# Attention, product of the probabilities with the values: key tiles 2, 3 before 0, 1, and the two row sums placed anew

## The chip, the core and the metric

The kernel runs on one core of one Trainium2 chip. The metric is the time of the whole program on the device in microseconds (us): before the change the median of three runs is 1252.38 us (1252.17 to 1255.42).

## What is computed

The reference is one block of a network on x of shape 8 x 512 x 128: a feed-forward part with routed experts, attention, and the same feed-forward part again. The change touches attention alone. Cut to what matters:

```python
b, n, _ = x.shape                     # 8, 512, 128;  HEADS = 16, DIM_HEAD = 64
qkv = x @ w_qkv.T
q, k, v = jnp.split(qkv, 3, axis=-1)  # each turned to (b, heads, n, 64)
q = q * cos + rotate_half(q) * sin + fenc
k = k * cos + rotate_half(k) * sin + fenc
dots = jnp.einsum('bhid,bhjd->bhij', q, k) * scale
attn = jax.nn.softmax(dots, axis=-1)
out = jnp.einsum('bhij,bhjd->bhid', attn, v)
return out @ w_out.T + b_out
```

## The kernel before

Attention goes in 64 steps, one for each of 8 batches times 8 pairs of heads. Such a step is called g. The five engines run a software pipeline of periods p = 0 to 63. In period p the work of several steps is under way: query and key of step p + 3 are projected and rotated, those of p + 2 are finished, the row maxima of p + 1 are taken, the scores of p are begun and those of p - 1 ended, p - 1 is multiplied with the values, and the output of p - 3 is projected and added to x. Every engine has its own list of instructions, written out by hand and kept in order by counting semaphores; nothing is reordered by a scheduler.

The probabilities of a step lie in `work` (`pt`): 4 tiles of 128 keys, each 128 x 1024 (both heads, 512 queries each). They serve twice. TensorE multiplies them with the values (`apply_v`, line 1184, 4 key tiles by 2 heads, 16 rows in the trace). And their sums over all keys are the softmax's denominators. For these, VectorE adds tile 1 onto tile 0 (`first_sum`, line 1383) and GpSimd adds tile 3 onto tile 2 (`second_sum`, line 1463), in place, so each may start only when `apply_v` has read its tiles. Then TensorE sums tiles 0 and 2 over the partitions (`denominators`, line 1201). `apply_v` signals `first_applied` behind its second tile and `o_ps` behind its last.

What else the period holds, by engine and in its order:

- TensorE: `apply_v` of p - 1 (L1184); the turn of the maxima of p + 1 (L1136); in every eighth period four transposes of the next batch (L1087); the projections of query and key of p + 3 (L1093); a tile of values (L1020); the output projection of p - 3 (L1211); `denominators` of p - 1 (L1201); then, as the first rows of the next period, four rounds of a product for the maxima (L1012) and one of scores (L1161, L1166). The second round of L1012 writes the bank that the output projection has left its result in, and so waits for VectorE's residual sum (`y_done`); the third and fourth wait for maxima that VectorE has taken.
- VectorE: four maxima (L1024), the reciprocals (L1379), a few small instructions of a layer norm, `first_sum` (L1383), the spread of the turned maxima (L1027), in every eighth period L1098, the two rotary products `turn` and `side` (L1362), the residual sum (L1391), and the next maxima.
- GpSimd: the output's scaling (L1470), two sums of the rotated parts (L1453, `turned_part`), `second_sum` (L1463), two low parts (L1458), two sums with the fourier term (L1447).
- SyncE issues the transfers. Four of them (L1541) move the partitions of `side` to `side_turned` as soon as VectorE has written it, and L1453 of the next period waits for them:

```python
                def turned_part(g, part, done, n):
                    pool.wait_ge(s["turned"], 64 * (g + 1))
                    pool.wait_ge(s["with_fourier"], 2 * g + n)
```

- ScalarE: the exponentials (L1291), the high parts of query and key (L1001), copies out of PSUM.

Of the kernel before, what the change touches and what calls it, by code (L numbers as in the profile page):

```python
# [20 lines left out]
B, T, D = 8, 512, 128  # L21
TT = T // P
# [68 lines left out]
def macaron(nc, x, w_gate_up, w_down, gate_t, w_qk, w_v, w_out, b_out, fproj, bproj,  # L91
            rope, fourier, consts, consts_b, codes, rows, out):
    with ExitStack() as ctx:
# [41 lines left out]
        pt = work[:, 4096:].rearrange("p (g k n) -> p g k n", g=2, k=TT)  # L135
# [731 lines left out]
        def attention():  # L867
# [11 lines left out]
            KQ, MT, XT = SA, SB[:, 0, 0:P], SB[:, 1, :]  # L879
            OWN = (slice(0, DH), slice(DH, P))  # L880
            Q, K = 0, 1
            N = B * PAIRS
            HALF = T // 2
            W_ALL = 3 + PAIRS + 2
# [26 lines left out]
            def exists(g):  # L911
                return 0 <= g < N
# [188 lines left out]
            def pe(pe, tail=None):  # L1101
# [66 lines left out]
                    ins.then_inc(s["scores"], 1)  # L1168

                def apply_v(g, kt):  # L1170
                    if kt == 0:
                        if not steady(g + 1):
                            pe.wait_ge(s["probs"], (g + 1) * TT)
                            pe.wait_ge(s["v_ready"], min(g + TT, B * 2 * TT))
                        if own_bank(g):
                            pe.wait_ge(s["maxes"], min((g + 2) * TT + 3, N * TT))
                        else:
                            pe.wait_ge(s["maxes"], min((g + 3) * TT, N * TT))
                            pe.wait_ge(s["y_done"], g - 2)
                        if not steady(g + 1):  # L1180
                            at_least(pe, s["o_copied"], g)
                    for h in range(2):
                        n = 2 * (g % PAIRS) + h
                        ins = nc.tensor.matmul(o_bank(g)[OWN[h], :], v_all[:, kt, n * DH:(n + 1) * DH],  # L1184
                                               pt[:, g % 2, kt, h * T:(h + 1) * T], start=(kt == 0), stop=(kt == TT - 1))
                    if kt == 1:
                        ins.then_inc(s["first_applied"], 1)
                    if kt == TT - 1:
                        ins.then_inc(s["o_ps"], 1)

                def denominators(g, p):
# [23 lines left out]
                def period(p):  # L1215
                    new, nxt, last = p + 3, p + 1, p - 1
                    if exists(nxt):
                        maxima(nxt, 0)
                    scores(last, 2)
                    if exists(nxt):  # L1220
                        maxima(nxt, 1)
                    scores(last, 3)
                    if exists(nxt):
                        maxima(nxt, 2)
                    scores(p, 0)
                    if exists(nxt):
                        maxima(nxt, 3)
                    scores(p, 1)
                    for kt in range(TT):
                        apply_v(last, kt)  # L1230
                    if exists(nxt):
                        turn_maxima(nxt, p)
                    if p == JOIN_LOGITS_AT:
                        ffn2["tensor"](pe, "logits")
                    if front_at(p) is not None:
                        pe.wait_ge(s["xn_ready"], front_at(p))
                        at_least(pe, s["probs"], p * TT + 1)
                        front(front_at(p), XT)
                    if exists(new) and new > 0:
                        project_both(new, p)  # L1240
                    if value_tile(p):
                        values(p)
                    if exists(p - 3):
                        project_out(p - 3, p)
                    if p == JOIN_FRONTS_AT:
                        pe.wait_ge(s["o_copied"], p)
                        ffn2["tensor"](pe, "fronts")
                    if exists(last) and p != JOIN_LOGITS_AT:
                        denominators(last, p)
# [13 lines left out]
                if tail is None:  # L1263
                    first_period()
                    for p in PERIODS[1:]:
                        period(p)
                    scores(N - 1, 2)
                    scores(N - 1, 3)
                    denominators(N - 2, N - 1)
                    ffn2["tensor"](pe, "turn")  # L1270
                    for kt in range(TT):
                        apply_v(N - 1, kt)
                elif tail == 0:
                    project_out(N - 3, N)
                elif tail == 1:
                    denominators(N - 1, N)
                elif tail == 5:
                    project_out(N - 2, N)
                elif tail == 10:
                    project_out(N - 1, N)  # L1280
# [75 lines left out]
            def dve(dve, tail=None):  # L1356
# [14 lines left out]
                def spread_maxima(g):  # L1371
                    dve.wait_ge(s["shift_ps"], g + 1)
                    at_least(dve, s["scores"], (g - 1) * TT)
                    spread(g, MT).then_inc(s["shift_ready"], 1)
# [4 lines left out]
                    nc.vector.reciprocal(rec_c[:, g % 2], den_c[:]).then_inc(s["rec_ready"], 1)  # L1379

                def first_sum(g):
                    dve.wait_ge(s["first_applied"], g + 1)
                    nc.vector.tensor_tensor(pt[:, g % 2, 0, :], pt[:, g % 2, 0, :], pt[:, g % 2, 1, :],  # L1383
                                            ALU.add).then_inc(s["first_sum"], 1)

# [16 lines left out]
                def period(p):  # L1402
                    new, nxt = p + 3, p + 1
                    if exists(nxt):
                        for qt in range(TT):
                            maxima(nxt, qt)
                    if exists(p - 2):
                        reciprocals(p - 2)
                    for n in LATE_SMALL_AT.get(p, ()):
                        small_step(n, LATER, mean_all, rs_all, shift_all)  # L1410
                    end_norm(p)
                    if p in JOIN_STATS_AT or p in JOIN_NORM_AT:
                        ffn2["vector"](dve, p)
                    if exists(p - 1):
                        first_sum(p - 1)
                    if exists(nxt):
                        spread_maxima(nxt)
                    if p == JOIN_FRONTS_AT:
                        ffn2["vector"](dve, "low")
                    if front_at(p) is not None:  # L1420
                        x_low(dve, front_at(p), XT)
                    if exists(new) and new > 0:
                        rope(new)
                    if exists(p - 3):
                        residual(p - 3)
# [18 lines left out]
            def pool(pool, early=None):  # L1444
# [14 lines left out]
                                                   ALU.subtract)  # L1459

                def second_sum(g):
                    pool.wait_ge(s["o_ps"], g + 1)
                    nc.gpsimd.tensor_tensor(pt[:, g % 2, 2, :], pt[:, g % 2, 2, :], pt[:, g % 2, 3, :],  # L1463
                                            ALU.add).then_inc(s["second_sum"], 1)

# [222 lines left out]
```

## Time and profile before

| | us |
|---|---|
| median of three runs | 1252.38 |
| the profiled execution's own time | 1252.67 |
| its span | 1250.9 |
| outside the span | 1.8 |
| TensorE (PE) busy | 1219.3 (97%) |
| VectorE (DVE) busy | 951.1 (76%) |
| GpSimd (POOL) busy | 907.2 (73%) |
| ScalarE (ACT) busy | 628.3 (50%) |

Busy shares are averages over three parts of the program that have different limits; attention's periods lie between about 250 and 1030 us. In the views that follow, a row of the timeline has the start, the duration, the engine, the line and what it writes from what it reads; behind that stands in brackets how long the engine had been idle before it, and what ended that wait.

### The profile page before, as it was taken

The numbers are of one execution on the slowest core, as the hardware profiler recorded it, in microseconds if no ns is written. First come the engines' busy times: TensorE is split into PE (matmuls) and PEld (weight loads), VectorE is DVE, ScalarE is ACT, GpSimd is POOL, SyncE is SP. The second block draws the span as 40 slices with busy tenths as digits, with TensorE's granted clock in tenths as the row PEclk, the third lists the DMA queues.
The fourth block names the chain that finished last, engine by engine and source line by source line (L and its number), as shares of the span: only waits on it lengthen the run. The fifth ranks groups of instructions, "written<-read, shape, count | busy, mean of one in ns | idle before, by whom it ended". The sixth has DMA issues, their size and how long they took to land.

```text
span 1250.9 us, 20277 instructions
## 1 busy us (share of the span) xinstructions
PE 1219.3 (97%) x7346; PEld 767.2 (61%) x7346; DVE 951.1 (76%) x1439; ACT 628.3 (50%) x921; POOL 907.2 (73%) x652
## 2 busy tenths in 40 slices
PE   5999999899999999999999999999999999999998
PEld 3666666566656566666656566666656556566665
DVE  6666787788988878887878888888888866666632
ACT  4444532565555546555555545555555564444422
POOL 0443446798998898898999899899989862543443
PEclk9999999999999999999999999999999999999999
DMA  5452141132323333232323323232323321443150
GB/s 172 136 186 64 73 136 34 34 70 52 78 53 70 60 64 66 60 70 52 74 57 73 57 64 66 60 70 53 75 55 72 58 44 20 143 144 94 60 161 17
DMA packets 118674, 95.30 MB, mean 76 GB/s; under 512 B 75760, under 2 KB 85008, under 8 KB 118320
## 3 DMA queue, kind: packets, MB, share of 16 engines
q1 hardware_dynamic: 118064, 93.75, 30.4%
q8 instruction: 59, 0.97, 0.3%
q14 instruction: 39, 0.32, 0.1%
q10 hardware_dynamic: 512, 0.26, 0.1%
HBM read 57.53 MB, written 2.88 MB: 48 GB/s over the span
## 4 chain that ended last, share of the span: by engine, by line
PE 81%; POOL 9%; issue 5%; DVE 3%; ACT 1%; DMA 1%; ACTq 0%; SPq 0%; POOLq 0%; DVEq 0%
PE banks L1184 15%; PE banks L455 15%; PE banks L1161 12%; PE banks L468 10%; PE banks L1093 6%; PE banks L1012 5%; PE banks L1201 4%; PE banks L1166 4%; PE banks L1211 3%; PE banks L1020 3%; POOL work L1463 3%; POOL turn L1453 2%; PE banks L1136 1%; POOL turn L1447 1%; POOL qk_l L1458 1%
## 5 line engine op out<-in xcount | busy, mean ns | idle before, releaser
L1024 DVE TENSOR_REDUCE neg_max<-banks 128x2 f32<-128x1024 f32 x256 | 301.4, 1226 | 13.5 <-PE banks L1012 10.0
L1291 ACT ACTIVATE work<-banks 128x1024 f32<-128x1024 f32 x256 | 262.4, 1027 | 88.3 <-PE banks L1166 64.7
L1184 PE MATMUL banks<-work 128*64 128x512 f32 x1024 | 233.8, 598 | 0.0
L1463 POOL TENSOR_TENSOR work<-work 128x1024 f32<-128x1024 f32 x64 | 160.5, 2508 | 60.4 <-PE banks L1184 60.4
L1453 POOL TENSOR_TENSOR turn<-turn,side_turned 128x512 f32<-128x512 f32 x128 | 173.9, 1380 | 30.7 <-DMA side_turned<-side 30.4
L1447 POOL TENSOR_TENSOR turn<-turn,fenc 128x512 f32<-128x512 f32 x128 | 163.1, 1296 | 1.8 <-DVE side L1362 1.8
L1458 POOL TENSOR_TENSOR qk_l<-turn,qk_h 128x512 fp32r<-128x512 f32 x128 | 162.0, 1287 | 0.1
L1184 PEld LDWEIGHTS banks<-work 128*64 128x64 f32 x1024 | 67.8, 136 | 132.7 <-issue 130.1
L1383 DVE TENSOR_TENSOR work<-work 128x1024 f32<-128x1024 f32 x64 | 105.7, 1652 | 33.3 <-PE banks L1184 33.1
L1001 ACT ACTIVATE qk_h<-turn 128x512 fp32r<-128x512 f32 x128 | 80.7, 631 | 96.0 <-POOL turn L1453 96.0
L816 POOL TENSOR_TENSOR o_raw<-o_raw,work 128x512 f32<-128x512 f32 x52 | 67.2, 1293 | 81.9 <-DVE o_raw L734 73.9
L816 POOL TENSOR_TENSOR work<-work 128x512 f32<-128x512 f32 x44 | 56.6, 1292 | 95.7 <-DVE work L734 53.5
L1012 PE MATMUL banks<-qk_h 64*128 64x512 f32 x512 | 109.8, 421 | 0.3 <-DVE neg_max L1024 0.2
L1161 PE MATMUL banks<-qk_h 64*128 64x512 f32 x512 | 102.9, 393 | 1.2 <-DVE side L1362 0.8
L1161 PE MATMUL banks<-qk_h,qk_l 64*128 64x512 f32 x512 | 102.7, 391 | 0.0
L1161 PE MATMUL banks<-qk_l,qk_h 64*128 64x512 f32 x512 | 102.3, 390 | 0.0
L1166 PE MATMUL banks<-shift,ones_r 64*128 64x512 f32 x512 | 102.3, 389 | 0.0
L1362 DVE TENSOR_TENSOR turn<-banks,rope_t 128x1024 f32<-128x1024 f32 x61 | 74.7, 1224 | 33.4 <-PE banks L1093 32.9
L1470 POOL TENSOR_TENSOR o_t<-o_raw,rec_all 128x512 f32<-128x512 f32 x64 | 83.0, 1296 | 22.4 <-DMA rec_all<-rec_d 22.4
L592 ACT ACTIVATE turn<-banks 128x512 f32<-128x512 f32 x80 | 47.8, 597 | 92.1 <-PE banks L455 90.7
L592 ACT ACTIVATE o_t<-banks 128x512 f32<-128x512 f32 x80 | 47.7, 597 | 87.0 <-PE banks L455 79.2
L455 PE MATMUL banks<-qk_h,gu_hi 128*128 128x512 f32 x160 | 87.6, 547 | 0.5 <-DVE o_raw L734 0.3
(178 smaller groups left out, 2440.5 us busy)
## 6 DMA issues: line engine op xcount, KB each, us to landing
work<-share SPq DMA_DIRECT2D x32, 1024.0 KB, 9.4
side_turned<-side SPq DMA_DIRECT2D x256, 128.0 KB, 3.1
rec_all<-rec_d SPq DMA_DIRECT2D x128, 128.0 KB, 3.0
x_tok<-in_x SPq DMA_DIRECT2D x8, 256.0 KB, 6.0
out<-x_tok SPq DMA_DIRECT2D x8, 256.0 KB, 9.6
work<-in_w_gate_up SPq DMA_DIRECT2D x1, 1280.0 KB, 7.1
work<-in_w_qk SPq DMA_DIRECT2D x1, 1024.0 KB, 12.6
den_d<-den_rows ACTq DMA_DIRECT2D x64, 4.0 KB
```

The costliest lines, as they stand in the source:

```text
L455: ins = nc.tensor.matmul(dst, w[:, j, :], a(b), start=(m == 0), stop=(m == 2))
L468: nc.tensor.matmul(Y[b % 2], down_w[:, g, :], hid(i), start=(i == first_of(b)), stop=(i == last_of(b))).then_inc(s["down"], 1)
L1012: ins = nc.tensor.matmul(to[:, h, :], qk_h[OWN[h], sets(g), Q, qt * P:(qt + 1) * P], qk_h[OWN[h], sets(g), K, :], start=True, stop=True)
L1024: return nc.vector.tensor_reduce(neg_max[:, g % 2, qt::DH], of, AX.X, ALU.max, negate=True)
L1161: nc.tensor.matmul(S[kt][:, h, :], k[OWN[h], sets(g), K, keys], q[OWN[h], sets(g), Q, :], start=(i == 0), stop=False)
L1166: ins = nc.tensor.matmul(S[kt][:, h, :], ones_r[OWN[h], :], shift[OWN[h], g % 2, :], start=False, stop=True)
L1184: ins = nc.tensor.matmul(o_bank(g)[OWN[h], :], v_all[:, kt, n * DH:(n + 1) * DH], pt[:, g % 2, kt, h * T:(h + 1) * T], start=(kt == 0), st ...
L1291: nc.scalar.activation(pt[:, g % 2, kt, :], S[kt].rearrange("p h q -> p (h q)"), ACT.Exp, scale=QSCALE).then_inc(s["probs"], 1)
L1447: nc.gpsimd.tensor_tensor(turn[:, g % 2, part], turn[:, g % 2, part], fenc[:], ALU.add).then_inc(s["with_fourier"], 1)
L1453: nc.gpsimd.tensor_tensor(turn[:, g % 2, part], turn[:, g % 2, part], side_turned[:, part], ALU.add).then_inc(done, 1)
L1458: return nc.gpsimd.tensor_tensor(qk_l[:, sets(g), part], turn[:, g % 2, part], qk_h[:, sets(g), part], ALU.subtract)
L1463: nc.gpsimd.tensor_tensor(pt[:, g % 2, 2, :], pt[:, g % 2, 2, :], pt[:, g % 2, 3, :], ALU.add).then_inc(s["second_sum"], 1)
```

## The change

The product with the values takes the key tiles in the order 2, 3, 0, 1. `first_applied` now comes when tiles 2 and 3 have been read, `o_ps` when all four have. GpSimd's `second_sum` of tiles 2 and 3 waits for `first_applied` in place of `o_ps`. VectorE's `first_sum` of tiles 0 and 1 waits for `o_ps` in place of `first_applied`, and moves behind `spread_maxima` in VectorE's order.

```diff
+            APPLIED = (2, 3, 0, 1)
...
                 def apply_v(g, kt):
-                    if kt == 0:
+                    if kt == APPLIED[0]:
...
-                                               pt[:, g % 2, kt, h * T:(h + 1) * T], start=(kt == 0), stop=(kt == TT - 1))
-                    if kt == 1:
+                                               pt[:, g % 2, kt, h * T:(h + 1) * T], start=(kt == APPLIED[0]),
+                                               stop=(kt == APPLIED[-1]))
+                    if kt == APPLIED[1]:
                         ins.then_inc(s["first_applied"], 1)
-                    if kt == TT - 1:
+                    if kt == APPLIED[-1]:
                         ins.then_inc(s["o_ps"], 1)
...
-                    for kt in range(TT):
+                    for kt in APPLIED:
                         apply_v(last, kt)
...
                 def first_sum(g):
-                    dve.wait_ge(s["first_applied"], g + 1)
+                    dve.wait_ge(s["o_ps"], g + 1)
...
                     if p in JOIN_STATS_AT or p in JOIN_NORM_AT:
                         ffn2["vector"](dve, p)
+                    if exists(nxt):
+                        spread_maxima(nxt)
                     if exists(p - 1):
                         first_sum(p - 1)
-                    if exists(nxt):
-                        spread_maxima(nxt)
...
                 def second_sum(g):
-                    pool.wait_ge(s["o_ps"], g + 1)
+                    pool.wait_ge(s["first_applied"], g + 1)
```

The same order of tiles holds for the last step, behind the loop. On VectorE, one period in the middle of attention stood like this before; `work<-work` is `first_sum`, `shift<-banks,own_rows` the spread, `turn` and `side` the rotary products, and the brackets name the semaphores waited for:

```order
L1379 RECIPROCAL rec_c<-den_c 128x8 [waits att_rec_out,att_den_in]
L288 TENSOR_TENSOR nt<-ve,rs 128x8 [waits dve_step_att]
L289 TENSOR_SCALAR nt<-rs 128x8
L1383 TENSOR_TENSOR work<-work 128x1024 [waits att_first_applied]
L1027 TENSOR_TENSOR shift<-banks,own_rows 128x512 [waits att_scores,att_shift_ps]
L1362 TENSOR_TENSOR turn<-banks,rope_t 128x1024 [waits att_turned,att_low,att_qk_ps]
L1362 TENSOR_TENSOR side<-banks,rope_t 128x1024
L1391 TENSOR_TENSOR x_tok<-banks,x_tok 128x512 [waits att_y_done,att_bias_added,att_y_ps]
```

The same place on VectorE with the change (its lines are numbered one or two higher):

```order
L1381 RECIPROCAL rec_c<-den_c 128x8 [waits att_rec_out,att_den_in]
L288 TENSOR_TENSOR nt<-ve,rs 128x8 [waits dve_step_att]
L289 TENSOR_SCALAR nt<-rs 128x8
L1028 TENSOR_TENSOR shift<-banks,own_rows 128x512 [waits att_scores,att_shift_ps]
L1385 TENSOR_TENSOR work<-work 128x1024 [waits att_o_ps]
L1364 TENSOR_TENSOR turn<-banks,rope_t 128x1024 [waits att_turned,att_low,att_qk_ps]
L1364 TENSOR_TENSOR side<-banks,rope_t 128x1024
L1393 TENSOR_TENSOR x_tok<-banks,x_tok 128x512 [waits att_y_done,att_bias_added,att_y_ps]
```

The sum and the spread have changed places; the rotary products stand directly behind the sum now.

On GpSimd, the same period before; `work<-work` is `second_sum`:

```order
L1470 TENSOR_TENSOR o_t<-o_raw,rec_all 128x512 [waits att_y_ps,att_o_copied,att_rec_in0]
L1453 TENSOR_TENSOR turn<-turn,side_turned 128x512 [waits att_with_fourier,att_turned] x2
L1463 TENSOR_TENSOR work<-work 128x1024 [waits att_o_ps]
L1458 TENSOR_TENSOR qk_l<-turn,qk_h 128x512 [waits att_k_high]
L1458 TENSOR_TENSOR qk_l<-turn,qk_h 128x512 [waits att_q_high]
```

And with the change:

```order
L1472 TENSOR_TENSOR o_t<-o_raw,rec_all 128x512 [waits att_y_ps,att_o_copied,att_rec_in0]
L1455 TENSOR_TENSOR turn<-turn,side_turned 128x512 [waits att_with_fourier,att_turned] x2
L1465 TENSOR_TENSOR work<-work 128x1024 [waits att_first_applied]
L1460 TENSOR_TENSOR qk_l<-turn,qk_h 128x512 [waits att_k_high]
L1460 TENSOR_TENSOR qk_l<-turn,qk_h 128x512 [waits att_q_high]
```

GpSimd's order is as it was; only the semaphore in front of its sum is another.

## Rows read from the trace of the kernel before

**Rows 1.** The page: busy time by engine, and the chain that ended last by engine.

```profile
PE 1219.3 (97%) x7346; PEld 767.2 (61%) x7346; DVE 951.1 (76%) x1439; ACT 628.3 (50%) x921; POOL 907.2 (73%) x652
...
PE 81%; POOL 9%; issue 5%; DVE 3%; ACT 1%; DMA 1%; ACTq 0%; SPq 0%; POOLq 0%; DVEq 0%
```

**Rows 2.** Timeline of TensorE: first rows of two products, 58 periods apart.

```profile
268.42 0.65 PE L1184 MATMUL banks<-work 128*64 128x512 f32 x2
...
1009.88 0.65 PE L1184 MATMUL banks<-work 128*64 128x512 f32 x2
```

**Rows 3.** The chain that ended last, one period: start, duration, what.

```profile
703.26 3.58 PE banks L1184 x16
...
710.10 1.00 PE banks L1201 x16
...
712.47 0.23 PE banks L1012 x2
...
715.95 1.43 PE banks L1184 x5
```

**Rows 4.** Timeline of VectorE in that period.

```profile
705.18 1.78 DVE L1383 TENSOR_TENSOR work<-work 128x1024 f32<-128x1024 f32 x1 [0.93 <-PE banks L1184]
707.14 0.69 DVE L1027 TENSOR_TENSOR shift<-banks,own_rows 128x512 fp32r<-128x512 f32 x1 [0.19 <-PE banks L1136]
708.55 1.22 DVE L1362 TENSOR_TENSOR turn<-banks,rope_t 128x1024 f32<-128x1024 f32 x1 [0.71 <-PE banks L1093]
709.69 1.22 DVE L1362 TENSOR_TENSOR side<-banks,rope_t 128x1024 f32<-128x1024 f32 x1
710.82 0.68 DVE L1391 TENSOR_TENSOR x_tok<-banks,x_tok 128x512 f32<-128x512 f32 x1
```

**Rows 5.** Timeline of GpSimd in that period.

```profile
703.36 2.52 POOL L1453 TENSOR_TENSOR turn<-turn,side_turned 128x512 f32<-128x512 f32 x2 [0.90 <-DMA side_turned<-side]
706.94 2.42 POOL L1463 TENSOR_TENSOR work<-work 128x1024 f32<-128x1024 f32 x1 [1.06 <-PE banks L1184]
709.31 2.54 POOL L1458 TENSOR_TENSOR qk_l<-turn,qk_h 128x512 fp32r<-128x512 f32 x2
...
716.04 2.52 POOL L1453 TENSOR_TENSOR turn<-turn,side_turned 128x512 f32<-128x512 f32 x2 [0.44 <-DMA side_turned<-side]
```

**Rows 6.** Line 1201: what ended TensorE's waits before it (us, times).

```profile
  POOL work L1463: 3.3, 5
```

**Rows 7.** Timeline: VectorE's sum beside GpSimd, in two other periods.

```profile
527.12 1.20 DVE L1383 TENSOR_TENSOR work<-work 128x1024 f32<-128x1024 f32 x1
527.44 3.14 POOL L1463 TENSOR_TENSOR work<-work 128x1024 f32<-128x1024 f32 x1 [1.07 <-PE banks L1184]
...
602.03 3.48 POOL L1453 TENSOR_TENSOR turn<-turn,side_turned 128x512 f32<-128x512 f32 x2 [1.33 <-DMA side_turned<-side]
603.13 1.25 DVE L1383 TENSOR_TENSOR work<-work 128x1024 f32<-128x1024 f32 x1 [0.69 <-PE banks L1184]
```

**Rows 8.** Chain and VectorE's timeline in a period with a late residual sum.

```profile
587.76 3.58 PE banks L1184 x16
...
597.48 0.49 PE banks L1012 x2
...
601.22 1.00 PE banks L1184 x3
...
596.65 0.68 DVE L1391 TENSOR_TENSOR x_tok<-banks,x_tok 128x512 f32<-128x512 f32 x1
```

**Rows 9.** Timeline: the longest way from `side` to GpSimd's next sum.

```profile
811.62 1.22 DVE L1362 TENSOR_TENSOR side<-banks,rope_t 128x1024 f32<-128x1024 f32 x1
812.86 3.88 SPq L1541 DMA_DIRECT2D side_turned<-side  x4
818.91 1.27 POOL L1453 TENSOR_TENSOR turn<-turn,side_turned 128x512 f32<-128x512 f32 x1 [1.38 <-DMA side_turned<-side]
```

**Rows 10.** Timeline of VectorE in a period with transposes.

```profile
388.05 0.69 DVE L1098 TENSOR_TENSOR x_lo<-banks,x_hi 128x512 fp32r<-128x512 f32 x1 [0.38 <-ACT x_hi L1285]
```

More of the change, by code:

```diff
@@ L1270, in pe @@
                     ffn2["tensor"](pe, "turn")
-                    for kt in range(TT):
+                    for kt in APPLIED:
                         apply_v(N - 1, kt)
```

## Prediction

> **What bounds the kernel now.** I read the page first: TensorE is busy for 97% of the span, and 81% of the chain that ended last is its work [rows 1]. Then the starts of the product with the values, period by period: from 268.42 to 1009.88 us there are 58 periods of 12.784 us in the mean [rows 2]. In one ordinary period the chain is TensorE alone, 703.26 to 715.95, or 12.69 us [rows 3]; here the others only have to be in time. So the question is how much room each has. I count from the start of the product in this period (t = 0 at 703.26) and read VectorE and GpSimd beside it.
>
> VectorE adds its tiles (L1383) from t = 1.92 to 3.70, spreads the maxima from 3.88 to 4.57, idles 0.71 us for TensorE's projections, and begins the rotary products at 5.29. `side` ends at 7.65, the residual sum runs from 7.56 to 8.24 [rows 4]. TensorE's second round of maxima, which needs that residual sum, starts at 9.21 [rows 3]: 0.97 us of room, less what a hand-over takes.
>
> GpSimd adds the rotated parts (L1453) from 0.10 to 2.62, waits 1.06 us for the product to end, and adds its tiles from 3.68 to 6.10. The start at 0.10 is set by the transfers of `side`: GpSimd had waited 0.90 us for them, and in the next period 0.44 us [rows 5]. From the end of `side` (709.69 + 1.22 = 710.91) [rows 4] to the next L1453 (716.04) [rows 5] passed 5.13 us. I call this L. I took it in 57 periods. In 35 of them GpSimd waited for the transfers, so L is their own: 5.13 (the least, some 12 times nearly the same) to 6.07 (812.84 to 818.91; there the four issues took 3.88 us) [rows 9], median 5.35, mean 5.45. In the other 22 it is only known from above; the mean of all 57 is 5.47.
>
> **What the order costs: the port.** VectorE's sum alone takes 1.20 us (527.12), and GpSimd's sum beside it 3.14 us in place of 2.42: it began to work when VectorE's was over [rows 5, 7]. The other way round, VectorE's sum behind a running L1453 ends 1.08 us after that (703.36 + 2.52 = 705.88, then 706.96) [rows 4, 5]. When the waiting sum fell between two L1453, it went in between, and the pair took 3.48 us in place of 2.52 [rows 5, 7]. So the two exclude each other for whole instructions, and a waiting VectorE sum goes before GpSimd's next instruction. The spread and the rotary products, which read PSUM, show no such lengthening [rows 4].
>
> **The change, part by part.**
>
> *Order of the tiles.* The same 16 rows of TensorE with the same signals at the same places: 0.
>
> *GpSimd's sum at half the product.* The wait of 1.06 us goes; the sum follows L1453 at once. What TensorE gains are its waits for this sum, 3.3 us in the whole program [rows 6]. That is the most that this part can bring.
>
> *VectorE's sum behind the spread.* Let x be the start of L1453 behind the start of the product (0.10 in this period). GpSimd's rows follow each other about 0.05 us before the modelled end (706.94 + 2.42 = 709.36, next at 709.31) [rows 5], VectorE's about 0.08 (709.69 + 1.22, next at 710.82) [rows 4].
> - GpSimd's sum then starts at x + 2.49 and ends at x + 4.91.
> - VectorE's sum is issued at 4.57 - 0.08 = 4.49. GpSimd's sum still runs, for every x above -0.4. So VectorE waits and ends at x + 4.91 + 1.08 = x + 5.99, while GpSimd's low parts are pushed back behind it.
> - The rotary products start at x + 5.91, not at 5.29: their wait for TensorE of 0.71 us covered only the first part. `side` starts 1.14 us on and ends at x + 8.27; the residual sum starts at x + 8.18 and ends at x + 8.86.
> - For what a late residual sum costs there are two periods before. In one it starts at 596.65, which is 8.89 us behind its product (587.76); TensorE's round follows 0.15 us behind its end, at 597.48, and the next product 4.57 us behind its start, at 601.22 [rows 8]. So the next product comes at x + 8.18 + 4.57 = x + 12.75.
>
> With x = 0.10 that alone would be 12.85, against 12.69: little. But `side` is late too, and it feeds the next x. The next L1453 starts at x + 8.27 + L, which counted from the next product is L - 4.48. This ring, transfers of `side`, two L1453, GpSimd's sum, VectorE's sum behind it, rotary products, transfers, takes 8.27 + L in a period: 13.40 us with L = 5.13, and more than TensorE's 12.69 with every L that was seen. Before the change the ring was open, since VectorE's sum stood ahead of the spread and the rotary products waited for TensorE only. Now it is the bound, and GpSimd's early sum is the piece in front of VectorE's.
>
> Is GpSimd itself fast enough for the ring? From the start of its sum to its next wait it needs 706.94 to 715.60, 8.66 us, with 2.49 for the L1453 pair and 1.08 for the lock 12.23: yes, it then waits some 1.4 us a period for transfers. `denominators` stands at 6.84 [rows 3] and needs VectorE's sum at x + 5.99; with x = 0.87 it is level, and later ones are hidden behind the residual sum. ScalarE's copies and the reciprocals have their cover in TensorE's longer period.
>
> *The sum.* I take L = 5.35: between the least, which is what the transfers need undisturbed, and the mean of all, which holds periods in which GpSimd and not the transfer was late. 58 x (8.27 + 5.35 - 12.784) = 58 x 0.836 = 48.5 us. In the seven periods with transposes L1098 stands behind VectorE's sum and ahead of the rotary products, and lengthens the ring by 0.69 - 0.08 = 0.61 us [rows 10]: 4.3 us. The 3.3 us of GpSimd's waits are already in the 12.784 and not counted again. Together 52.8 us on the profiled time of 1252.67: 1305.5, and since that execution lies 0.3 us above the median, **1305.2 us**. Ends: L = 5.13 gives 58 x 0.616 + 4.3 = 40.0, so 1292; L = 5.47 gives 59.8, so 1312.
>
> [...]
>
> **The rivals.**
> - *Ring (forecast)*, 1292 to 1312: 0.83.
> - *No ring, a shift only*: the transfers get shorter when TensorE's stalls have moved the other transfers away from them, below 4.6 us, and x stays near 0.10. Then a period is 12.85, 0.07 above the mean, with the seven transposes 58 x 0.07 + 4.3: 1261 us. Against it: 5.13 is a hard floor in the rows. 0.04.
> - *Not slower*: the port isn't contended for by the two large sums (no row shows VectorE's behind GpSimd's large one), and VectorE's sum takes 1.20 us. It ends at 5.69, the residual sum starts at 7.88, and 7.88 + 4.57 = 12.45 is under 12.69; `side` ends at 7.97, x rises to 0.4, nothing follows. The 3.3 us of rows 6 come back: 1249 us. It decides where VectorE's sum ends before 5.93. For it speaks nothing but that gap; against it GpSimd's 3.14 us [rows 7]. 0.06.
> - *VectorE first*: if L is so long in some periods that the second L1453 still runs at 4.49 (x above 2), VectorE's sum goes ahead of GpSimd's, and such a period ends 0.5 us earlier. L would have to be 6.5; where it happens in one period in ten it saves 3 us: 1302. 0.02.
> - *The hand-over of the port is slow* behind the large sum, like a semaphore's (0.15 us behind the end, rows 8, and then the full 1.20): the ring is 0.27 us longer, 15.7 us in all: 1321. 0.02.
> - *Issues collide*: the four transfers now start about 0.9 us later in the period and meet the copy of the denominators more often; all L near 5.9: 58 x 1.386 + 4.3 = 84.7, 1337 us. 0.03.
>
> **How the numbers follow.** The likeliest case spans 1292 to 1312. Its other terms are read from rows to some 0.07 us, 4 us in 58 periods: 1288 below. Above I go to 1319, towards the slow hand-over and the mild part of the collisions. That leaves out the shift alone, the case that is not slower, the hard collisions, and a little of the rest, less than 0.2. A measurement of this kernel tells about 0.3% (3.8 us) from no change. Slower by more: 0.83 + 0.04 + 0.02 + 0.02 + 0.03 = 0.94. The case that is not slower lies at 1249, 0.26% below, and falls on either side of that bound: same 0.04, faster 0.02.
>
> **What would show it.** Right: the VectorE sum (now L1385) lasts about 2.4 us in nearly every period and ends 1.08 us behind GpSimd's; GpSimd waits for `side_turned` in every period, about 1.4 us (0.90 and 0.44 in [rows 5]), and no more for the product; the chain that ended last runs over VectorE, transfers and GpSimd through attention; the product starts every 13.4 to 14.1 us, and TensorE waits about 0.8 us a period at the second round of maxima; busy times per instruction on TensorE and the granted clock stay. Wrong: sums of 1.2 us at the same place (the port), periods of 12.8 us with late residual sums (the ring), or an L outside 5.1 to 6.1. The prediction fails most easily in L, since 0.1 us of it is 6 us of the result.

## The result, and the profile after the change

The changed kernel takes 1314.62 us (median of five runs, 1310.42 to 1314.86) against 1252.36 us before (median of five, 1251.79 to 1255.42): a ratio of 1.0485, with a 95% interval of 1.0468 to 1.0502. It is 62 us slower; the forecast was 1305.2 us, 53 slower, in a range of 1288 to 1319. The profiled execution of the changed kernel is the fastest of the five, 1310.42 us with a span of 1308.6 us; all sizes below that come from its trace are for 57.7 us more span.

The page of the changed kernel, to be read beside [rows 1]: TensorE has the same 7346 instructions and is busy for a smaller share, and the chain has moved from TensorE and GpSimd to VectorE.

```profile
span 1308.6 us, 20277 instructions
PE 1237.1 (95%) x7346; PEld 779.6 (60%) x7346; DVE 984.1 (75%) x1439; ACT 624.2 (48%) x921; POOL 944.1 (72%) x652
...
PE 61%; DVE 19%; issue 15%; DMA 2%; POOL 1%; ACT 1%; SPq 1%; DVEq 0%; POOLq 0%; ACTq 0%
```

The first rows of the product, as in [rows 2], 58 periods apart on TensorE's timeline:

```profile
273.77 0.65 PE L1185 MATMUL banks<-work 128*64 128x512 f32 x2
...
1065.85 0.65 PE L1185 MATMUL banks<-work 128*64 128x512 f32 x2
```

That is 792.08 us, 13.657 us a period in place of 12.784: 50.6 us of the 57.7. The rest is found below, in one period ahead of these and in one behind them.

One ordinary period, as in [rows 4] and [rows 5], its product starting at 356.17 in the chain. VectorE's timeline:

```profile
360.05 0.69 DVE L1028 TENSOR_TENSOR shift<-banks,own_rows 128x512 fp32r<-128x512 f32 x1 [1.88 <-PE banks L1137]
360.66 2.17 DVE L1385 TENSOR_TENSOR work<-work 128x1024 f32<-128x1024 f32 x1
362.75 1.21 DVE L1364 TENSOR_TENSOR turn<-banks,rope_t 128x1024 f32<-128x1024 f32 x1
363.88 1.21 DVE L1364 TENSOR_TENSOR side<-banks,rope_t 128x1024 f32<-128x1024 f32 x1
365.01 0.68 DVE L1393 TENSOR_TENSOR x_tok<-banks,x_tok 128x512 f32<-128x512 f32 x1
```

GpSimd's timeline in the same period:

```profile
356.88 2.50 POOL L1455 TENSOR_TENSOR turn<-turn,side_turned 128x512 f32<-128x512 f32 x2
359.32 2.41 POOL L1465 TENSOR_TENSOR work<-work 128x1024 f32<-128x1024 f32 x1
361.68 3.54 POOL L1460 TENSOR_TENSOR qk_l<-turn,qk_h 128x512 fp32r<-128x512 f32 x2
365.18 2.54 POOL L1449 TENSOR_TENSOR turn<-turn,fenc 128x512 f32<-128x512 f32 x2
...
370.84 1.27 POOL L1455 TENSOR_TENSOR turn<-turn,side_turned 128x512 f32<-128x512 f32 x1 [1.85 <-DMA side_turned<-side]
```

The reader is to see four things ("the port" stands here, as in the prediction, for what VectorE's sum and GpSimd's instructions can't use at the same time, by these rows). VectorE's sum is issued at 360.66 and ends at 362.83, that is 1.10 us behind the end of GpSimd's (361.73). It isn't this period alone: from 273.8 to 1066 us the one ends 1.08 to 1.09 us behind the other in 57 of 58 periods. GpSimd's two low parts take 3.54 us in place of 2.54: the first stood behind VectorE's sum. The rotary products have no bracket any more: nothing but the sum holds them. And from the end of `side` (365.09) to the next L1455 (370.84) pass 5.75 us; this is one of the longer L.

That the loop closes shows in the lengths of the periods. In the 50 periods without transposes from 301 us to the end of the 58, the length of a period less the L just ahead of it is 8.17 to 8.25 us, 8.21 in the mean, while L itself runs from 5.16 to 6.13: whatever L has more, the next period has more. Before the change the same difference scatters from 6.8 to 7.7 us.

The chain through the same period, which ran over TensorE alone in [rows 3]:

```profile
356.17 3.59 PE banks L1185 x16
359.75 0.27 PE banks L1137
...
360.66 0.85 DVE work L1385
361.51 1.24 issue
362.75 0.32 DVE turn L1364
363.07 0.81 issue
363.88 1.21 DVE side L1364
365.09 0.61 DVE x_tok L1393
365.70 0.14 issue
365.83 0.50 PE banks L1013 x2
...
369.61 1.43 PE banks L1185 x5
```

"issue" is time in which, for the profile, nothing was waited for. It is no sign of the port: `turn`, which wasn't held (1.21 us), has 0.81 us of it too. The profile names no releaser for the wait for the port, so only the length of the sum's row shows it, beside GpSimd's row. The residual sum ends at 365.69, TensorE's second round of maxima follows at 365.83.

### The profile page after: what moved, and what is told of

Its sections match the earlier page's. It is cut to its first block, busy times and chain, and to the rows that moved or that the text cites. A ratio compares the mean times of both kernels' runs of the same rounds, so it can differ in the third digit from the quotient of the medians.

```text
span 1308.6 us, 20277 instructions
## 1 busy us (share of the span) xinstructions
PE 1237.1 (95%) x7346; PEld 779.6 (60%) x7346; DVE 984.1 (75%) x1439; ACT 624.2 (48%) x921; POOL 944.1 (72%) x652
## 4 chain that ended last, share of the span: by engine, by line
PE 61%; DVE 19%; issue 15%; DMA 2%; POOL 1%; ACT 1%; SPq 1%; DVEq 0%; POOLq 0%; ACTq 0%
PE banks L1185 16%; PE banks L455 14%; PE banks L1162 10%; PE banks L468 9%; DVE side L1364 5%; PE banks L1013 5%; DVE work L1385 4%; PE banks L1167 3%; DVE x_tok L1393 3%; DVE turn L1364 3%; PE banks L1137 1%; DMA den_c<-den_d 1%; DVE shift L1028 1%; SPq L1543 1%; PE banks L410 1%
## 5 line engine op out<-in xcount | busy, mean ns | idle before, releaser
L1025 DVE TENSOR_REDUCE neg_max<-banks 128x2 f32<-128x1024 f32 x256 | 295.2, 1209 | 7.2 <-PE banks L1013 7.2
L1455 POOL TENSOR_TENSOR turn<-turn,side_turned 128x512 f32<-128x512 f32 x128 | 160.5, 1275 | 85.8 <-DMA side_turned<-side 85.5
L1460 POOL TENSOR_TENSOR qk_l<-turn,qk_h 128x512 fp32r<-128x512 f32 x128 | 221.6, 1750 | 0.1
L1465 POOL TENSOR_TENSOR work<-work 128x1024 f32<-128x1024 f32 x64 | 153.4, 2397 | 13.3 <-PE banks L1185 13.3
L1385 DVE TENSOR_TENSOR work<-work 128x1024 f32<-128x1024 f32 x64 | 146.1, 2283 | 3.8 <-PE banks L1185 3.8
L1013 PE MATMUL banks<-qk_h 64*128 64x512 f32 x512 | 118.3, 442 | 28.5 <-DVE x_tok L1393 28.3
L1028 DVE TENSOR_TENSOR shift<-banks,own_rows 128x512 fp32r<-128x512 f32 x64 | 44.2, 691 | 120.5 <-PE banks L1137 120.2
L1162 PE MATMUL banks<-qk_h 64*128 64x512 f32 x512 | 107.1, 397 | 1.0 <-DVE side L1364 0.8
L1162 PE MATMUL banks<-qk_l,qk_h 64*128 64x512 f32 x512 | 105.2, 392 | 0.0
L1013 PEld LDWEIGHTS banks<-qk_h 64*128 64x128 f32 x512 | 51.2, 185 | 87.2 <-issue 81.2
L592 ACT ACTIVATE o_t<-banks 128x512 f32<-128x512 f32 x80 | 47.8, 597 | 86.0 <-PE banks L455 79.8
## 6 DMA issues: line engine op xcount, KB each, us to landing
work<-in_w_qk SPq DMA_DIRECT2D x1, 1024.0 KB, 12.6
```

The costliest lines, as they stand in the source:

```text
L1013: ins = nc.tensor.matmul(to[:, h, :], qk_h[OWN[h], sets(g), Q, qt * P:(qt + 1) * P], qk_h[OWN[h], sets(g), K, :], start=True, stop=True)
L1025: return nc.vector.tensor_reduce(neg_max[:, g % 2, qt::DH], of, AX.X, ALU.max, negate=True)
L1162: nc.tensor.matmul(S[kt][:, h, :], k[OWN[h], sets(g), K, keys], q[OWN[h], sets(g), Q, :], start=(i == 0), stop=False)
L1455: nc.gpsimd.tensor_tensor(turn[:, g % 2, part], turn[:, g % 2, part], side_turned[:, part], ALU.add).then_inc(done, 1)
L1460: return nc.gpsimd.tensor_tensor(qk_l[:, sets(g), part], turn[:, g % 2, part], qk_h[:, sets(g), part], ALU.subtract)
```

## The experiments

Ten kernels were run. "Period" is the mean over the same 58 periods as above, from the first rows of the product in each trace; before it is 12.784, after the change 13.657. A ratio is to the kernel before as it was timed beside that run (its medians were 1252.25 to 1254.60 us); differences in us from the changed kernel are from its 1314.62, timed beside 1252.36, and are good to 2 or 3 us.

**Does the port hold VectorE's sum, or is it only late?** In place of VectorE's sum a maximum over tile 0, in the same place, with one input from SBUF. Tile 1 is left out of the denominators, so this kernel computes something else and is there for its time only:

```diff
-                    nc.vector.tensor_tensor(pt[:, g % 2, 0, :], pt[:, g % 2, 0, :], pt[:, g % 2, 1, :],
-                                            ALU.add).then_inc(s["first_sum"], 1)
+                    nc.vector.tensor_reduce(one_in[:, g % 2, :], pt[:, g % 2, 0, :].rearrange("p (h q) -> p h q", h=2),
+                                            AX.X, ALU.max, negate=True).then_inc(s["first_sum"], 1)
```

> The changed kernel in which VectorE's sum of tiles 0 and 1 is replaced by a maximum over tile 0 (same 128 x 1024 read, same place, same waits, 4 bytes times 2 written; so tile 1 is left out of the denominators). It has one input from SBUF, not two. Theory (the port): it does not wait for GpSimd, lasts 1.2 us, ends at 5.8 behind the product's start, and the ring opens: 1250 to 1258 us, plus what the small layer norm steps near 255 us still cost (up to 7). Rival (what stands late in the period is late, whatever it reads): 1310 us as the changed kernel.

Measured: 1254.99 us, ratio to before 1.0021 (1.0004 to 1.0038); period 12.758. Its line in this kernel, over all 64 steps (duration in ns: least, median, most):

```profile
L1386 DVE TENSOR_REDUCE one_in<-work x64: 1201/1209/1220, 246.5 to 1049.2; 128x2 f32<-128x1024 f32 x64
```

The same view of the sum in the changed kernel:

```profile
L1385 DVE TENSOR_TENSOR work<-work x64: 1207/2168/3091, 245.7 to 1105.4; 128x1024 f32<-128x1024 f32 x64
```

In both kernels GpSimd's sum was already running in 60 of the 64 places when VectorE's instruction began; the sum is lengthened, the maximum never. With that the whole loss in the ordinary periods is gone, so the new place and the new signals cost nothing by themselves there. The rival "late is late" is refuted. What in the instruction makes the difference is less sure. The maximum has one input less, and it also writes next to nothing; the rotary products write all of 128 x 1024 to SBUF from one input in PSUM and one in SBUF and aren't held either (1.20 to 1.21 us in the changed kernel), so the write alone isn't it. And one input isn't always enough, as the period of 19 us below shows; in this kernel too that period is long, 17.3 us.

**Is it the place behind the spread?** VectorE's sum put back ahead of it, all else as changed:

```diff
-                    if exists(nxt):
-                        spread_maxima(nxt)
                     if exists(p - 1):
                         first_sum(p - 1)
+                    if exists(nxt):
+                        spread_maxima(nxt)
```

> The changed kernel with VectorE's sum put back ahead of the spread; it still waits for the whole product, and GpSimd's sum still starts at half of it. Theory (port and ring): the sum is issued while GpSimd's sum runs and again ends about 1.1 us behind it, now with the spread (0.6 us) between it and the rotary products; the ring is 0.6 us longer, about 14.2 us a period, in all up to 35 us over the changed kernel: 1335 to 1350 us; less where GpSimd is so late that VectorE's sum goes first. Rival (the place behind the spread is what costs): back to 1252 to 1262 us.

Measured: 1321.75 us, ratio 1.0527 (1.0482 to 1.0573); period 13.90. Slower than the changed kernel, so the place behind the spread isn't what costs; but 13 us below the range that I gave. Two of its periods, on VectorE's timeline:

```profile
360.04 2.99 DVE L1385 TENSOR_TENSOR work<-work 128x1024 f32<-128x1024 f32 x1 [1.66 <-PE banks L1185]
...
374.01 1.29 DVE L1385 TENSOR_TENSOR work<-work 128x1024 f32<-128x1024 f32 x1 [1.00 <-PE banks L1185]
```

and on GpSimd's:

```profile
359.54 2.40 POOL L1465 TENSOR_TENSOR work<-work 128x1024 f32<-128x1024 f32 x1
...
374.18 3.37 POOL L1465 TENSOR_TENSOR work<-work 128x1024 f32<-128x1024 f32 x1
```

In the first VectorE waits for GpSimd's sum; in the second it was issued 0.17 us before GpSimd's started, went first, and GpSimd's took 3.37 us. It was so in 16 of the 58 periods, which last 13.3 us in the mean, the others 14.1. I had named the escape and given it too little weight.

One period of this kernel, 17.6 us long, doesn't fit the rule of the prediction that a waiting VectorE sum goes before GpSimd's next instruction. Its rows on VectorE's and on GpSimd's timeline:

```profile
1023.51 6.13 DVE L1385 TENSOR_TENSOR work<-work 128x1024 f32<-128x1024 f32 x1 [2.29 <-PE banks L1185]
...
1023.72 2.39 POOL L1465 TENSOR_TENSOR work<-work 128x1024 f32<-128x1024 f32 x1
1026.07 2.48 POOL L1460 TENSOR_TENSOR qk_l<-turn,qk_h 128x512 fp32r<-128x512 f32 x2
```

VectorE's sum was issued ahead of all three of GpSimd's and ended 1.09 us behind the last of them. Why, no run shows.

**Does GpSimd's early start matter?** Its sum waits for the whole product again:

```diff
-                    pool.wait_ge(s["first_applied"], g + 1)
+                    pool.wait_ge(s["o_ps"], g + 1)
```

> The changed kernel, GpSimd's sum waits for the whole product again (as before the change); order of tiles and VectorE's place as changed. Theory (port): GpSimd's sum runs from 3.7 to 6.1 in every period, VectorE's behind it to 7.2, the next product 6.7 us later: 13.9 us a period in place of 13.66, so about 1329 us, with little wait for transfers. Rival (GpSimd's early start is what disturbs): less than the changed kernel, 1253 to 1275 us.

Measured: 1338.89 us, ratio 1.0675 (1.0643 to 1.0707). An ordinary period on GpSimd's and on VectorE's timeline:

```profile
362.18 2.40 POOL L1465 TENSOR_TENSOR work<-work 128x1024 f32<-128x1024 f32 x1 [0.49 <-PE banks L1185]
...
362.99 2.67 DVE L1385 TENSOR_TENSOR work<-work 128x1024 f32<-128x1024 f32 x1
```

Again VectorE's sum ends 1.08 us behind GpSimd's (365.66 and 364.58). Ordinary periods are 13.91 us, as expected; the mean is 14.036, and the total 10 us above my figure: I had set the ordinary 13.9 against the changed kernel's mean, in which the seven long periods with transposes (14.5 here) are contained. "With little wait for transfers" was wrong: GpSimd waits 1.39 us a period for them and, in the period shown, 0.49 us more for the product. So of the change's parts GpSimd's early start helps, by 24 us, once VectorE's sum stands behind it.

**Are the transfers on the path?** One small transfer more ahead of the four of `side`, in the changed kernel and in the one before:

```diff
+                    if g >= 3:
+                        sp.dma_start(extra_d[g], ident[0:32, 0:8]).then_inc(extra, 16)
```

> The changed kernel with one small transfer more (1 KB, to memory that nothing reads) issued on SyncE ahead of the four of side, in each period. Theory (ring through the transfers): L grows by one issue, 0.5 to 0.6 us, and each of 58 periods with it: 29 to 35 us over the changed kernel, about 1346 us. Rival (the periods are long only because the sum is late within its period, transfers are hidden): 1315 us, within 3 us.

> The kernel before with the same small transfer ahead of the four of side. Theory: the ring is open here, so only periods in which GpSimd is already late get longer: 5 to 15 us, 1257 to 1267 us, well under half of what the same edit costs in the changed kernel. Rival (an issue costs the same anywhere): 29 to 35 us here as well.

Measured: after the change 1332.6 us (ratio 1.0629, 1.0604 to 1.0655), 18.0 us more than without it, period 14.016, 0.36 longer; before the change 1264.07 us (ratio 1.0074, 1.0052 to 1.0096), 11.7 us more than its 1252.36 and 9.5 more than the 1254.60 timed beside it, period 12.996, 0.21 longer. SyncE's timeline in the first:

```profile
410.45 0.33 SPq L1543 DMA_DIRECT2D extra_d<-ident  x1
410.82 3.54 SPq L1547 DMA_DIRECT2D side_turned<-side  x4
```

The small transfer moves the four by 0.37 us, not by 0.5 to 0.6, and the changed kernel's period grows by just that: one for one, as on a ring. The rival of hidden transfers is refuted. The kernel before pays 0.21 of it, 0.6 of the changed kernel's and not under half. It was nearer to its edge than I said: TensorE's waits for GpSimd's sum ahead of `denominators`, 3.3 us in 5 places in [rows 6], are here

```profile
  POOL work L1465: 12.5, 20
```

and its waits there for a copy of ScalarE's grew from 7.2 to 18.5 us.

**Does opening the ring help?** The two rotary products exchanged, with a signal of its own for `side`, which SyncE now waits for; in the changed kernel and in the one before:

```diff
-                    for to, part in ((turn[:, g % 2], 0), (side[:], 1)):
-                        ins = nc.vector.tensor_tensor(to, KQ, rope_t[:, part:part + 1, :].broadcast_to([P, QK, T]), ALU.mult)
-                    ins.then_inc(s["roped"], 1)
+                    for to, part, done in ((side[:], 1, "side_done"), (turn[:, g % 2], 0, "roped")):
+                        nc.vector.tensor_tensor(to, KQ, rope_t[:, part:part + 1, :].broadcast_to([P, QK, T]),
+                                                ALU.mult).then_inc(s[done], 1)
```

> The changed kernel with the two rotary products exchanged: side is written first and signals SyncE by itself, turn second. The same instructions. Theory (ring): the transfers leave 1.14 us earlier, the ring is 7.13 + L and no longer longer than TensorE's 12.69 in ordinary periods; what is left is VectorE's sum that waits for the port: 1275 to 1300 us, 1290 as one number. Rival (transfers are not in the bound): 1312 to 1317 us as the changed kernel.

> The kernel before with the two rotary products exchanged. Theory: GpSimd is no longer late for its sum, TensorE's waits for it (3.3 us) go: 1248 to 1250 us. Rival (those waits have another cause, or turn, now second, is late for GpSimd): 1252 us or above.

Measured: on the changed kernel 1292.2 us (ratio 1.0316, 1.029 to 1.0342), period 13.359, 22 us less than without it. On the kernel before 1249.66 us, ratio 0.997 (0.9956 to 0.9983), period 12.737: the fastest of all, and faster than before beyond the interval, by 0.3%. TensorE's waits for GpSimd's sum at line 1201 there, 3.3 us in [rows 6]:

```profile
  POOL work L1463: 1.6, 2
```

Both numbers came as forecast, though the waits at line 1201 fell by half and didn't go. The 13.359 is what is left when the transfers are off the path: GpSimd comes earlier, in 31 of the 58 periods VectorE's sum ends 2.33 us behind GpSimd's, that is behind the first low part too, and in 23 it still ends 1.08 us behind.

**Could VectorE take both sums?** On the kernel before, tiles 2 and 3 are added on VectorE too, at the end of the product and ahead of the spread, and GpSimd has no sum:

```diff
                     if exists(p - 1):
                         first_sum(p - 1)
+                        second_sum(p - 1)
```

> The kernel before with both sums on VectorE: tiles 0, 1 at half the product, tiles 2, 3 at its end, ahead of the spread; GpSimd has none. Theory: VectorE has the room (0.8 us before the second round of maxima waits), the port is held 2.4 us a period less by GpSimd: 1248 to 1252 us. Rival (VectorE becomes late in many periods): 1256 us or above.

Measured: 1297.7 us, ratio 1.0356 (1.0334 to 1.0378), period 13.568. A miss of 46 us. VectorE's timeline in two neighbouring periods (L1388 is the second sum):

```profile
299.94 1.23 DVE L1383 TENSOR_TENSOR work<-work 128x1024 f32<-128x1024 f32 x1
301.66 1.73 DVE L1388 TENSOR_TENSOR work<-work 128x1024 f32<-128x1024 f32 x1 [0.49 <-PE banks L1184]
...
312.67 2.33 DVE L1383 TENSOR_TENSOR work<-work 128x1024 f32<-128x1024 f32 x1
314.93 2.31 DVE L1388 TENSOR_TENSOR work<-work 128x1024 f32<-128x1024 f32 x1
```

and GpSimd's low parts in the second of them:

```profile
313.88 4.50 POOL L1465 TENSOR_TENSOR qk_l<-turn,qk_h 128x512 fp32r<-128x512 f32 x2
```

I had counted how long GpSimd holds the port and not how often. In the second period each of VectorE's sums waits for one GpSimd instruction, since GpSimd no longer pauses for the product: 1.20 became 2.3. Over the whole kernel the median is 1.42 us for the first sum and 2.31 for the second. The second sum ends at 317.24, and the rotary products start at 317.76, 7.1 us behind the start of the product (310.69), where they stood at 5.29 before. The period of the first two rows took 12.7 us, that of the other two 13.9.

**What is the period of 19 us?** In the trace after the change the product that starts at 254.7 is followed by the next only at 273.8: 19.1 us, 12.6 before. It holds six small layer norm instructions (128 x 20) on VectorE, five steps by the program's count, since one step has two. Its timeline:

```profile
256.80 0.98 DVE L293 SCALAR_TENSOR_TENSOR rs<-nt 128x20 f32<-128x20 f32 x1
257.81 1.21 DVE L288 TENSOR_TENSOR nt<-ve,rs 128x20 f32<-128x20 f32 x1
258.94 0.16 DVE L289 TENSOR_SCALAR nt<-rs 128x20 f32<-128x20 f32 x1
259.14 2.25 DVE L291 TENSOR_TENSOR nt<-nt,rs 128x20 f32<-128x20 f32 x1
261.43 1.19 DVE L293 SCALAR_TENSOR_TENSOR rs<-nt 128x20 f32<-128x20 f32 x1
262.64 1.18 DVE L1042 SCALAR_TENSOR_TENSOR shift_all<-mean,rs 128x20 f32<-128x20 f32 x1
263.75 0.68 DVE L1028 TENSOR_TENSOR shift<-banks,own_rows 128x512 fp32r<-128x512 f32 x1
```

They take 7.0 us where the work of one is under 0.2; the one of 2.25 us spans GpSimd's whole sum, those of 1.2 one of its smaller instructions each. Before the change the last four of them fell into GpSimd's pause ahead of its sum (one row of VectorE's timeline, one of GpSimd's):

```profile
258.26 0.18 DVE L291 TENSOR_TENSOR nt<-nt,rs 128x20 f32<-128x20 f32 x1
...
259.56 2.69 POOL L1463 TENSOR_TENSOR work<-work 128x1024 f32<-128x1024 f32 x1 [1.45 <-PE banks L1184]
```

In the kernel with the one-input maximum one of them, of another kind and with a single tensor input, waits out GpSimd's whole sum as well:

```profile
257.65 2.43 DVE L290 TENSOR_SCALAR nt<-rs 128x20 f32<-128x20 f32 x1
...
257.65 2.40 POOL L1466 TENSOR_TENSOR work<-work 128x1024 f32<-128x1024 f32 x1
```

In the changed kernel the spread comes at 263.75, 5 us late. TensorE stands idle behind it for 5.14 us, and then its 16 rows of `denominators` take 1.93 us, where they took 1.00 in [rows 3]:

```profile
265.81 1.93 PE L1203 MATMUL banks<-work,ones_f 128*32 128x256 f32 x16 [5.14 <-DVE work L1385]
```

Its granted clock, 1.00 in all of attention before, falls to the lower of its levels (1.2 GHz in place of 2.4) for part of the stretch (the columns are the stretch, its length, busy times of PE, PEld, DVE, ACT, POOL, granted clock, share and GB/s of the transfers):

```profile
254.00:275.00 21.00, 15.86 (x95) 8.83 (x94) 17.16 (x18) 8.62 (x12) 13.65 (x11) 0.84 0.25 50
```

Two edits tested that, both on the changed kernel: the nine last steps dealt out over three periods, and then the last five moved away from that period.

```diff
-LATE_SMALL_AT = {1: range(7, 11), 2: range(11, LN_STAGES)}
+LATE_SMALL_AT = {1: range(7, 10), 2: range(10, 13), 3: range(13, LN_STAGES)}
```

> The changed kernel, with the nine last small steps of the layer norm dealt out over periods 1, 2, 3 (3 each) in place of 4 and 5 over periods 1, 2. Theory: in the profile of the changed kernel one period near 255 us took 19.1 us, since six such steps waited one after the other for the port behind a GpSimd that no longer pauses (7 us), and TensorE's clock fell to half behind that pause; with fewer in one period that goes: 5 to 7 us less than the changed kernel, about 1308 us. Rival (the long period is the pipeline's start): no less than 1312 us.

Measured: 1309.62 us, ratio 1.0454 (1.0435 to 1.0473), 5 us less; but the period is still 18.9 us in its profile, since the four instructions left there took 5.8 us from the first's start to the last's end. So the forecast time came and its mechanism didn't, and 5 us are hardly more than the 4.4 us by which the changed kernel's own runs spread. The second edit:

```diff
-LATE_SMALL_AT = {1: range(7, 11), 2: range(11, LN_STAGES)}
+LATE_SMALL_AT = {1: range(7, 11), 3: range(11, LN_STAGES)}
```

> The changed kernel with the last five small layer norm steps moved from period 2 to period 3, so that period 2, the one of 19.1 us, has none (dealing them out, 4 in that period, left it at 18.9 us: each still waited for one GpSimd instruction). Theory: every such step waits about 1.2 us or more for the port in that period, so with none it falls to 14 to 15 us and the clock does not drop: 1306 to 1310 us against the changed kernel's 1310 to 1315, if period 3 does not inherit the wait. Rival (start of the pipeline): the period stays at 18 to 19 us.

Measured: 1311.94 us, ratio 1.0474 (1.0446 to 1.0503). The period without the steps is 13.5 us, the one that has them now 19.5, and the lower clock went with them: 0.86 in the 25 us from 275, 1.00 in the 25 us before. So the steps are the cause, not the start of the pipeline. Moving them saves 2.7 us, less than the runs spread, and the time lies above the 1306 to 1310 expected: the wait went with them, since GpSimd doesn't pause where they stand now either.

What took GpSimd's pause away there isn't the new signal alone. In the changed kernel L1455 begins at 256.47, 1.8 us behind the start of its product, after a wait of 1.86 us for transfers, so the product is over before GpSimd's sum could start. And in the kernel where that sum waits for the whole product again this period is as long, 19.3 us. The late transfers are enough. In the kernel with the maximum L1456 begins 0.4 us behind that start, and there it is the early signal that takes the pause.

## Why the prediction was right, point by point

- *Order of the tiles, no cost*: right. With the one-input instruction everything else of the change is in place, and the period is 12.758, against 12.784 before.
- *Two large sums exclude each other, a waiting sum ends 1.08 us behind the other and goes before GpSimd's next instruction*: right, 1.08 to 1.09 in 57 of 58 periods of the changed kernel and in all 58 of the one with GpSimd's sum late; against it stands the one period of 6.13 us. The Trainium skill (SBUF — State Buffer, "A bandwidth-pool intuition that's wrong") has a figure for another pair, a DMA whose descriptors GpSimd can't write while VectorE holds the port: blocked until VectorE's end plus about 115 ns. Carried over to the sum, as an estimate, that would be 1.20 + 0.115 = 1.32 us behind; the runs show 1.08.
- *The ring of 8.27 + L*: right, with 8.21 for 8.27. In a clean period the product-to-product time is 13.37 to 13.44 with L = 5.17 to 5.19; L = 5.16 to 6.13 over 57 periods, in the mean 5.38, where 5.35 was taken. The 58 periods gave 50.6 us, where 52.8 was forecast for them with their transposes. That 5.13 is "a hard floor in the rows" was misread: in two of the periods before in which GpSimd didn't wait for the transfers the whole way took 4.98 and 5.05 us (from `side`'s end at 327.26 and 506.02), so the transfers took no longer than that. Both the one-for-one cost of an issue and the gain of 22 us when `side` goes first fit this ring and none of the rivals.
- *Transposes, 0.61 us each*: right, 13.97 to 14.01 us for six of the seven such periods beside 13.4; the seventh, behind a longer L, took 14.40.
- *What VectorE does ahead of the spread*: this is the term that was missing. I called the reciprocals covered and priced nothing else there, and the period with the six small instructions got 6.5 us longer, with the clock's fall. [rows 5] held the warning: GpSimd's pause, 1.06 us there, was also time in which VectorE's small instructions found the port free, and both the early signal and late transfers take it away.
- *The end of attention*: the period that starts at 1065.9 took 14.4 us, 12.2 before, part of it at the lower clock. I had taken the transition at nothing. It and the long period, less 1.1 and 0.5 us that the start and the rest of the program came out shorter, are the 7.1 us between 50.6 and 57.7.
- *The signs*: VectorE's sum lasts 2.17 us in the median, 2.4 was said; GpSimd waited for `side_turned` 55 times between 268 and 1070 us, 79.8 us in all, and once, 0.2 us, for the product; in the periods the clock stayed, and so did TensorE's rows but for L1013 (439 ns in place of 419). Two signs were off. TensorE waits 0.49 us a period at its second round of maxima (28.3 us in 58), 0.8 was said; another 8.9 us lie ahead of `denominators`. And the chain that ended last runs over VectorE, but not over transfers and GpSimd (DMA 2%, POOL 1%): the link from GpSimd's sum to VectorE's has no releaser in the profile, so the chain can't follow the ring there. The ring is shown by the lengths of the periods and by the experiments.
- *The number itself*: 1305.2 against 1314.62. Of the 9.4 us, 4.9 are profiled (57.7 against 52.8): 7.1 that I hadn't priced, less 2.2 by which the periods were priced too high, so a small part is luck. Another 4.2 are that the profiled run, at 1310.42, is the fastest of five, and 0.3 is the median before. In what the slower ones differ no trace shows; it stays open.
- *The rivals*: "not slower" fell with VectorE's sum, 2.17 us in the median and not 1.20; "a shift only" with the mean L of 5.38; the slow hand-over with 1.08; collisions happened, but not often: L was 5.9 or more in 6 of 57 periods, in 4 of 57 of those before in which GpSimd waited for the transfers. "VectorE first" was seen, but only where VectorE's sum is issued earlier, in the kernel with the sum ahead of the spread.

## What to carry to other kernels

Before a VectorE instruction that GpSimd can hold up is moved (here sums of two SBUF inputs, and small instructions with one or two), look at what GpSimd runs at the new place, and count its instructions, not only their time: each such VectorE instruction can wait for a whole one, in one case even for three, and a chain of small dependent ones waits once each. A pause of GpSimd in the trace may be what keeps VectorE short. And when a step that feeds a transfer gets later, follow the transfer to its reader and on: if the way leads back to the step, the delay isn't paid once in a period but sets the period.

## What the runs showed of the hardware

- A wait for the port leaves no releaser in the profile. It shows as a longer row (2.17 us for 1.20). "issue" in the chain doesn't tell it: it stands behind held and free instructions alike (1.24 us with the sum, 0.81 with `turn`).
- VectorE's maximum over 128 x 1024 fp32 with one SBUF input lasted 1.20 to 1.22 us in all 64 places, in 60 of them with GpSimd's sum running when it began; the sum with two inputs, at the same place in the changed kernel, 1.21 to 3.09 us.
- The sum, once held, ended 1.08 to 1.09 us behind GpSimd's in 57 of 58 periods, less than the 1.20 us that it takes alone. Issued 0.02 to 0.69 us ahead of GpSimd's it went first in 16 periods of the kernel with the sum ahead of the spread, and once (0.21 us ahead) it waited for three GpSimd instructions, 6.13 us.
- Small steps aren't spared: 128 x 20 elements took 2.25 us when GpSimd's sum was running, and 0.17 us when it wasn't; one with a single tensor input (TENSOR_SCALAR, 128 x 20) took 2.43 us beside GpSimd's sum in the kernel with the one-input maximum, and 0.16 us at 258.94 in the changed kernel, between two GpSimd instructions.
- TensorE's granted clock fell (0.84 in the mean over 21 us) in the long period, where it had stood idle for 5.14 us, and again behind waits of 0.75 and 1.27 us at the end of attention (0.94 over 1065 to 1092 us, 1.00 at that place before). Over 268 to 1066 us its mean is 1.00, though TensorE stood idle there for 0.64 us a period in the mean.
